# Attention: the value products of a unit in two halves, and the steps behind them one slot later

## The chip, the cores and the metric

The kernel runs on one core of a Trainium2 chip. The metric is the device time of one execution in microseconds; the kernel before was run three times.

## The reference

The input is `x` of 8 x 512 x 256 and a context of the same shape. Four blocks follow each other, each added to `x`: an mLSTM mixing block over 4 heads, a GELU network, a cross-attention over 16 heads of 64, and a router with 8 experts. The change lies in the attention:

```python
q = query @ W_Query + B_Query          # 256 -> 1024, 16 heads of 64
k = key @ W_Key + B_Key
v = value @ W_Value + B_Value
scores = jnp.einsum('bqhd,bkhd->bhqk', q, k) / D ** 0.5
probs = jax.nn.softmax(scores, axis=-1)
out = jnp.einsum('bhqk,bkhd->bqhd', probs, v)
return out.reshape(B, Lq, H * D) @ W_Output + B_Output
```

The query is the normalized `x`, key and value are the context.

## The kernel before

`attention` (from line 827) works in 64 units `u`, one for each pair of heads of each of the 8 batches (HP = 8 pairs a batch). A unit has 2 heads x 4 tiles of 128 query rows, so 8 row tiles, and an iteration of the loop over `u` has 8 slots `j`, one for each. There are 65 iterations: each engine's program runs the same double loop, with the later steps of unit u - 1 and the first steps of unit u + 1 beside the slots of unit u. The order of each engine's queue is written out by hand in these loops, and an engine works its queue in order.

What a slot j of iteration u does, by engine:

- **TensorE.** `score(u, j)`: two matmuls of 512 columns (line 958), into one of two PSUM banks. `turn(u, j - 2)`: four transposes (line 969) of the scaled row tile two slots back, into one of two banks; slots 0 and 1 do those of tiles 6 and 7 of unit u - 1. Then, by slot: 0 and 1, `project(u + 1, ...)` of queries and keys (line 937); 2, all of `weigh_values(u - 1)` (line 979); 4, `project_values(u + 1)` (line 946); 5 and 6, a half each of `output(u - 1, ...)` (line 989). `weigh_values` multiplies, for each of 4 key tiles and 2 heads, a 128 x 64 block of values with 512 columns of turned probabilities; the heads go to the two halves of the columns of the array and of one bank (O_BANK). Each f32 matmul is two instructions in the trace.
- **VectorE.** `row_sum(u, j - 1)` (a reciprocal, line 1158), `row_max(u, j)` (line 1153), `keep(u, j - 2)` (line 1165, a copy of the turned tile out of PSUM), and by slot: 1, the second part of the queries (line 1140, two instructions); 2, that of the keys (line 1147); 7, both halves of `add_out(u - 1, ...)` (line 1172), which add the output products to x. Half 1 of the output shares O_BANK with the value products.
- **ScalarE.** The exponential of tile j with its row sum (line 1093); queries in slot 0 and keys in slot 1, out of PSUM; `heads_out` in slot 4, before the exponential (line 1070); `values` in slot 5 (line 1065); and the copies of turned tiles 4 and 5 in slots 6 and 7 (line 1112).
- **GpSimd.** It multiplies each row tile with its reciprocal (line 1128).
- **SyncE.** After each unit's keys it issues four transfers that copy the keys between partitions (line 913).

So a row tile passes this chain: score, row maximum (VectorE), exponential (ScalarE), reciprocal (VectorE), scaling (GpSimd), turn (TensorE).

From the second batch on, four iterations of each eight (u % 8 = 1 to 4, u >= 8) also treat the batch that is done. NORM (1): VectorE takes statistics, one tile in each of slots 2 to 5. APPLY (2): VectorE normalizes, one tile in each of slots 2 to 5. TURN (3): TensorE transposes in slots 3 and 7; ScalarE copies the first part in slot 4 and the second in slot 0 of the next iteration, after the exponential. GATE (4): TensorE multiplies with the gate weights in slots 3 and 7, and `project` of the keys in slot 1 waits for the second of those copies (semaphore `xT`), as it writes the same bank. The last batch is treated after the loop.

The waits of TensorE's steps, as far as they matter: `turn(u, j)` waits for the scaled tile (`pn`) and for a free bank; `score(u, j)` for exponential j - 2; `weigh_values(u - 1)` for all turned tiles of its unit and for the last addition that read O_BANK (`x`).

Of the kernel before, what the change touches and what calls it, by code (L numbers as in the profile page):

```python
# [24 lines left out]
TPB = S // P  # L25
# [338 lines left out]
def wait_count(eng, sem, value):  # L364

    if value > 0:
        eng.wait_ge(sem, value)
# [459 lines left out]
def attention(nc, c, x_all, xnT_all, ctxT_all, first, Wq, Wk, Wv, Wo, gate_w, lg, rows, rows_in, out, landed):  # L827

    U = HP * B
    NBL = 2 * TPB  # L830
    with ExitStack() as ctx:
# [8 lines left out]
        V = sb("V", [P, 2, TPB, P], F32)  # L840
# [24 lines left out]
        def there(u):  # L865
            return 0 <= u < U
# [15 lines left out]
        def wait_turned_copies(eng, u, n):  # L882

            wait_count(eng, s["pt_v"], u * BY_DVE[NBL] + BY_DVE[n])
            wait_count(eng, s["pt_a"], u * BY_ACT[NBL] + BY_ACT[n])

        with nc.Block() as block:
# [32 lines left out]
            def _(pe):  # L920
# [49 lines left out]
                                           c["ident"][:, :])  # L970
                    ins.then_inc(s["t_ps"], 1)

                def weigh_values(u):
                    wait_turned_copies(pe, u, NBL)
                    pe.wait_ge(s["V"], u + 1)
                    wait_count(pe, s["x"], 2 * u)
                    for t in range(TPB):
                        for h in range(2):
                            ins = pe.matmul(ps[AD * h:AD * h + AD, O_BANK, :], V[:, u % 2, t, AD * h:AD * h + AD],  # L979
                                            PT[:, u % 2, h, t, :], start=t == 0, stop=t == TPB - 1)  # L980
                    ins.then_inc(s["pv"], 1)

                def output(u, half):
                    if half == 0:
# [32 lines left out]
                for u in range(U + 1):  # L1017
                    for j in range(NBL):
                        if there(u):
                            score(u, j)  # L1020
                            if j >= 2:
                                turn(u, j - 2)
                        if j < 2 and there(u - 1):
                            turn(u - 1, NBL - 2 + j)
                        if j < 2 and there(u + 1):
                            project(u + 1, j)
                        if j == 2 and there(u - 1):
                            weigh_values(u - 1)
                        if j == 4 and there(u + 1):
                            project_values(u + 1)  # L1030
                        if j in (5, 6) and there(u - 1):
                            output(u - 1, j - 5)
                        if j in (3, 7) and there(u):
                            if j == 3 and there(u + 1) and u % HP in (TURN, GATE):
                                pe.wait_ge(s["kl"], u + 2)
                            if routed(u, TURN) is not None:
                                turn_rows(routed(u, TURN), j // 4)
                            if routed(u, GATE) is not None:
                                if routed(u, GATE) == 0 and j == 3:
                                    pe.wait_ge(s["gT"], 16 * DC)  # L1040
                                map_gates(routed(u, GATE), j // 4)
# [6 lines left out]
            def _(act):  # L1048
# [36 lines left out]
                values(0)  # L1085
                for u in range(U + 1):
                    for j in range(NBL):
                        if j == 4 and there(u - 1):
                            heads_out(u - 1)
                        if there(u):  # L1090
                            act.wait_ge(s["nmax"], NBL * u + j + 1)
                            wait_count(act, s["t_ps"], NBL * u + j - 3)
                            act.activation(Pr[:, j % 4, :], ps[:, S_BANK + j % 2, :], ACT.Exp,  # L1093
                                           bias=nmax[:, j % 4:j % 4 + 1], accum_out=rsum[:, j % 4:j % 4 + 1]
                                           ).then_inc(s["exp"], 1)
                        if j == 4 and routed(u, TURN) is not None:
                            keep_rows(routed(u, TURN), 0)
                        if j == 0 and routed(u, TURN + 1) is not None:
                            keep_rows(routed(u, TURN + 1), 1)
                        if j == 0 and routed(u, GATE + 1) is not None:  # L1100
                            keep_logits(routed(u, GATE + 1))
                        if there(u + 1):
                            if j == 0:
                                queries(u + 1)
                            if j == 1:
                                keys(u + 1)
                            if j == 5:
                                values(u + 1)
                        if there(u) and j - 2 in ON_ACT:
                            act.wait_ge(s["t_ps"], NBL * u + j - 1)  # L1110
                            q = P * ((j - 2) % TPB)
                            act.copy(PT[:, u % 2, (j - 2) // TPB, :, q:q + P],
                                     ps[:, T_BANK + j % 2, :].rearrange("p (t q) -> p t q", t=TPB)
                                     ).then_inc(s["pt_a"], 1)
# [20 lines left out]
            def _(dve):  # L1135
# [72 lines left out]
                for u in range(U + 1):  # L1208
                    for j in range(NBL):
                        if there(u):  # L1210
                            if j >= 1:
                                row_sum(u, j - 1)
                            row_max(u, j)
                            if j >= 2:
                                keep(u, j - 2)
                        if j < 2 and there(u - 1):
                            keep(u - 1, NBL - 2 + j)
                        if there(u + 1):
                            if j == 1:
                                queries(u + 1)  # L1220
                            if j == 2:
                                keys(u + 1)
                        if 2 <= j < 2 + TPB and routed(u, NORM) is not None:
                            take_stats(routed(u, NORM), j - 2)
                        if j == 2 + TPB and routed(u, NORM) is not None:
                            finish_stats(routed(u, NORM))
                        if 2 <= j < 2 + TPB and routed(u, APPLY) is not None:
                            apply(routed(u, APPLY), j - 2)
                        if j == 7:
                            if there(u):  # L1230
                                row_sum(u, j)
                            if there(u - 1):
                                if u > 1:
                                    dve.wait_ge(s["x"], 2 * (u - 1))
                                add_out(u - 1, 0)
                                add_out(u - 1, 1)
                for t in range(TPB):
                    take_stats(LAST, t)
                finish_stats(LAST)
# [500 lines left out]
```

## Time and profile before

| | us |
|---|---|
| runs | 1843.49, 1844.89, 1848.96 |
| median | 1844.89 |
| span of the profiled execution | 1843.2 |
| TensorE busy | 1663.1 (90%) |
| VectorE busy | 1209.8 (66%) |
| ScalarE busy | 843.8 (46%) |
| GpSimd busy | 608.1 (33%) |

The page gives only the span of the profiled execution, from first to last instruction; its own time was not taken apart from it. The attention stage takes from about 437 to 1655 us. In rows of a timeline stand the start, the time covered, the engine, the line and operation, the tiles, and how many instructions the row merges; in brackets is the engine's idle time before the first and what ended it. PE is the matmuls and PEld the weight loads of TensorE, DVE is VectorE, ACT ScalarE, POOL GpSimd. An instruction can start while the one before it on its engine ends, so the distance between starts is what an instruction costs its engine.

### The profile page before, as it was taken

The page shows a single profiled execution, that of the slowest core. Times are in us where ns is not written, and L with a number is a line of the kernel's source. Part 1 is how long each engine was busy: PE and PEld are TensorE (multiplying, and loading weights), DVE is VectorE, ACT ScalarE, POOL GpSimd, SP SyncE. Part 2 cuts the span into 40 slices and gives each one's busy share as a digit, 9 for nine tenths or more (in the row PEclk, how much of TensorE's full clock was granted, in tenths as well). Part 3 has the DMA queues.
Part 4 walks back from the last instruction along what each step waited for, and adds up shares of the span by engine and source line. Part 5 has one row for each costly group of instructions (what it writes and reads, how often), then busy time and mean ns, then how long its engine had stood idle before and what let it go on. Part 6 is the DMA issues. An engine that isn't in the chain of part 4 may idle for free. (4 is left out here: it accounts for less than half of the span.)

```text
span 1843.2 us, 25796 instructions
## 1 busy us (share of the span) xinstructions
PE 1663.1 (90%) x8789; PEld 1128.1 (61%) x8789; DVE 1209.8 (66%) x2689; ACT 843.8 (46%) x1870; POOL 608.1 (33%) x730
## 2 busy tenths in 40 slices
PE   6569999996999999999999999999999999973584
PEld 4447777754666666666666666666666766642352
DVE  6445656532777777776776776776777677757761
ACT  3324343431555555555555555555555555531110
POOL 2143445430333323332332332333232323220375
PEclk9669999997999999999999999999999999985697
DMA  8100000003323232323232322222223223213254
GB/s 254 27 23 12 12 12 1 1 0 106 69 47 69 47 92 46 69 69 69 47 92 47 67 72 61 54 65 74 56 60 79 59 53 86 46 45 99 44 85 58
DMA packets 68961, 109.46 MB, mean 59 GB/s; under 512 B 18400, under 2 KB 50400, under 8 KB 68832
## 3 DMA queue, kind: packets, MB, share of 16 engines
q1 hardware_dynamic: 62688, 99.29, 22.1%
q0 software_dynamic: 6144, 8.52, 3.0%
q8 instruction: 72, 1.18, 0.3%
q14 instruction: 57, 0.47, 0.1%
HBM read 27.84 MB, written 12.85 MB: 22 GB/s over the span
## 5 line engine op out<-in xcount | busy, mean ns | idle before, releaser
L1128 POOL TENSOR_SCALAR at_Pr<-at_Pr,at_rinv 128x512 f32<-128x512 f32 x512 | 355.8, 695 | 841.2 <-DVE at_rinv L1158 841.2
L1093 ACT ACTIVATE at_Pr<-at_ps,at_nmax 128x512 f32<-128x512 f32 x512 | 352.2, 688 | 535.2 <-DVE at_nmax L1153 533.6
L1153 DVE TENSOR_REDUCE at_nmax<-at_ps 128x1 f32<-128x512 f32 x512 | 351.2, 686 | 154.0 <-PE at_ps L958 142.5
L958 PE MATMUL at_ps<-at_k,at_q 128*128 128x512 f32 x1024 | 420.7, 492 | 10.8 <-DMA at_k<-at_k_own 9.1
L969 PE MATMUL at_ps<-k_ident,at_Pr 128*128 128x128 f32 x2048 | 309.8, 274 | 4.5 <-POOL at_Pr L1128 4.5
L969 PEld LDWEIGHTS at_ps<-k_ident,at_Pr 128*128 128x128 f32 x2048 | 250.5, 140 | 90.2 <-POOL at_Pr L1128 27.7
L1165 DVE COPY at_PT<-at_ps 128x512 f32<-128x512 f32 x384 | 261.4, 681 | 0.0
L958 PEld LDWEIGHTS at_ps<-at_k,at_q 128*128 128x128 f32 x1024 | 174.6, 191 | 130.7 <-issue 121.2
L979 PE MATMUL at_ps<-at_PT,at_V 128*64 128x512 f32 x1024 | 235.4, 602 | 0.9 <-DVE at_PT L1165 0.9
L1158 DVE RECIPROCAL at_rinv<-at_rsum 128x1 f32<-128x1 f32 x512 | 83.3, 163 | 161.1 <-ACT at_Pr L1093 159.1
L979 PEld LDWEIGHTS at_ps<-at_PT,at_V 128*64 128x64 f32 x1024 | 68.1, 137 | 122.5 <-issue 121.4
L989 PE MATMUL at_ps<-at_wo,at_oT 128*128 128x256 f32 x512 | 131.6, 380 | 0.8 <-ACT at_oT L1070 0.8
L459 PE MATMUL mm_ps<-mx_w,mm_hT 128*128 128x256 f32 x512 | 119.6, 382 | 0.0
L449 PE MATMUL mm_ps<-m_xnT,mx_w 128*128 128x512 f32 x256 | 112.6, 598 | 1.3 <-ACT m_xnT L598 1.3
L937 PE MATMUL at_ps<-m_ctxT,at_w_rest 128*128 128x512 f32 x224 | 105.9, 595 | 4.0 <-ACT m_xnT L1075 4.0
L946 PE MATMUL at_ps<-at_w_rest,m_ctxT 128*128 128x128 f32 x896 | 109.2, 275 | 0.0
L937 PE MATMUL at_ps<-m_xnT,at_w_rest 128*128 128x512 f32 x224 | 107.1, 601 | 0.0
L946 PEld LDWEIGHTS at_ps<-at_w_rest,m_ctxT 128*128 128x128 f32 x896 | 104.5, 192 | 0.0
L459 PEld LDWEIGHTS mm_ps<-mx_w,mm_hT 128*128 128x128 f32 x512 | 94.3, 190 | 16.1 <-issue 3.8
L1140 DVE SCALAR_TENSOR_TENSOR at_q<-at_ps,m_b_all,at_q 64x512 fp32r<-64x512 f32 x128 | 96.0, 750 | 11.0 <-ACT at_q L1053 8.2
L1093 ACT ACTIVATION_READ_ACCUMULATOR at_Pr<-at_ps,at_nmax 128x1 f32 x512 | 98.5, 192 | 0.0
L989 PEld LDWEIGHTS at_ps<-at_wo,at_oT 128*128 128x128 f32 x512 | 87.4, 190 | 8.3 <-ACT at_oT L1070 1.7
(236 smaller groups left out, 1996.5 us busy)
## 6 DMA issues: line engine op xcount, KB each, us to landing
at_k<-at_k_own SPq DMA_DIRECT2D x256, 256.0 KB, 4.3
k_x<-in_x SPq DMA_DIRECT2D x8, 512.0 KB, 8.5
mg_ctx<-in_ctx SPq DMA_DIRECT2D x8, 512.0 KB, 8.7
mx_ctxn<-in_ctx SPq DMA_DIRECT2D x8, 512.0 KB, 3.8
rows<-m_ctxT SPq DMA_DIRECT2D x16, 256.0 KB, 2.6
out<-k_x SPq DMA_DIRECT2D x8, 512.0 KB, 3.5
r_w<-in_L_ffn_w SPq DMA_DIRECT2D x16, 256.0 KB, 5.5
mx_w<-in_L_ffn_w SPq DMA_DIRECT2D x2, 1024.0 KB, 10.0
```

The source lines that it names most:

```text
L449: ins = pe.matmul(ps[:, H_BANK + f % 4, :], w1_s[:, k, P * f:P * f + P], xnT_all[:, k, b * S:b * S + S], start=k == 0, stop=k == DC - 1)
L459: ins = pe.matmul(ps[:, Y_BANK + t // 2, D * (t % 2):D * (t % 2) + D], hT[:, f, P * t:P * t + P], w2_s[:, f, :], start=f == 0, stop=f == F ...
L937: ins = pe.matmul(ps[:, A_BANK + k, :], weights(k, d, hp), src[:, d, b * S:b * S + S], start=d == 0, stop=d == DC - 1)
L946: ins = pe.matmul(ps[:, A_BANK, P * t:P * t + P], ctxT_all[:, d, b * S + P * t:b * S + P * t + P], weights(2, d, hp), start=d == 0, stop=d ...
L958: ins = pe.matmul(ps[:, S_BANK + j % 2, :], q2[:, u % 2, h, q:q + P], k2[:, u % 2, h, part, :], start=part == 0, stop=part == 1)
L969: ins = pe.transpose(ps[:, T_BANK + j % 2, P * t:P * t + P], Pr[:, j % 4, P * t:P * t + P], c["ident"][:, :])
L979: ins = pe.matmul(ps[AD * h:AD * h + AD, O_BANK, :], V[:, u % 2, t, AD * h:AD * h + AD], PT[:, u % 2, h, t, :], start=t == 0, stop=t == TP ...
L989: ins = pe.matmul(ps[:, Y_BANK - half, D * (t % 2):D * (t % 2) + D], oT[:, P * t:P * t + P], wo_s[:, u % HP, :], start=True, stop=True)
L1093: act.activation(Pr[:, j % 4, :], ps[:, S_BANK + j % 2, :], ACT.Exp, bias=nmax[:, j % 4:j % 4 + 1], accum_out=rsum[:, j % 4:j % 4 + 1]).th ...
L1128: pool.tensor_scalar(Pr[:, n % 4, :], Pr[:, n % 4, :], rinv[:, n % 4:n % 4 + 1], 1.0, ALU.mult, ALU.mult).then_inc(s["pn"], 1)
L1153: dve.tensor_reduce(nmax[:, j % 4:j % 4 + 1], ps[:, S_BANK + j % 2, :], AX.X, ALU.max, negate=True).then_inc(s["nmax"], 1)
L1165: dve.tensor_copy(PT[:, u % 2, j // TPB, :, q:q + P], ps[:, T_BANK + j % 2, :].rearrange("p (t q) -> p t q", t=TPB)).then_inc(s["pt_v"], 1)
```

## The change

The value products of unit u - 1 are made in two halves: key tiles 0 and 1 in slot 2, tiles 2 and 3 in slot 4. (The short name counts slots from 1.) The value projection goes from slot 4 to slot 5, the halves of the output products from slots 5 and 6 to 6 and 7. ScalarE's `heads_out` goes to slot 5 and `values` to slot 6. VectorE's second addition to x goes from the end of slot 7 to slot 0 of the next iteration, behind the row maximum and the copy of a turned tile there.

```diff
--- before.py
+++ after.py
@@ -970,15 +970,17 @@
                                            c["ident"][:, :])
                     ins.then_inc(s["t_ps"], 1)
 
-                def weigh_values(u):
-                    wait_turned_copies(pe, u, NBL)
-                    pe.wait_ge(s["V"], u + 1)
-                    wait_count(pe, s["x"], 2 * u)
-                    for t in range(TPB):
+                def weigh_values(u, half):
+                    if half == 0:
+                        wait_turned_copies(pe, u, NBL)
+                        pe.wait_ge(s["V"], u + 1)
+                        wait_count(pe, s["x"], 2 * u)
+                    for t in (2 * half, 2 * half + 1):
                         for h in range(2):
                             ins = pe.matmul(ps[AD * h:AD * h + AD, O_BANK, :], V[:, u % 2, t, AD * h:AD * h + AD],
                                             PT[:, u % 2, h, t, :], start=t == 0, stop=t == TPB - 1)
-                    ins.then_inc(s["pv"], 1)
+                    if half:
+                        ins.then_inc(s["pv"], 1)
 
                 def output(u, half):
                     if half == 0:
@@ -1024,12 +1026,12 @@
                             turn(u - 1, NBL - 2 + j)
                         if j < 2 and there(u + 1):
                             project(u + 1, j)
-                        if j == 2 and there(u - 1):
-                            weigh_values(u - 1)
-                        if j == 4 and there(u + 1):
+                        if j in (2, 4) and there(u - 1):
+                            weigh_values(u - 1, j // 4)
+                        if j == 5 and there(u + 1):
                             project_values(u + 1)
-                        if j in (5, 6) and there(u - 1):
-                            output(u - 1, j - 5)
+                        if j in (6, 7) and there(u - 1):
+                            output(u - 1, j - 6)
                         if j in (3, 7) and there(u):
                             if j == 3 and there(u + 1) and u % HP in (TURN, GATE):
                                 pe.wait_ge(s["kl"], u + 2)
@@ -1085,7 +1087,7 @@
                 values(0)
                 for u in range(U + 1):
                     for j in range(NBL):
-                        if j == 4 and there(u - 1):
+                        if j == 5 and there(u - 1):
                             heads_out(u - 1)
                         if there(u):
                             act.wait_ge(s["nmax"], NBL * u + j + 1)
@@ -1104,7 +1106,7 @@
                                 queries(u + 1)
                             if j == 1:
                                 keys(u + 1)
-                            if j == 5:
+                            if j == 6:
                                 values(u + 1)
                         if there(u) and j - 2 in ON_ACT:
                             act.wait_ge(s["t_ps"], NBL * u + j - 1)
@@ -1233,7 +1235,11 @@
                                 if u > 1:
                                     dve.wait_ge(s["x"], 2 * (u - 1))
                                 add_out(u - 1, 0)
-                                add_out(u - 1, 1)
+                        if j == 0 and there(u - 2):
+                            wait_count(dve, s["x"], 2 * (u - 2))
+                            add_out(u - 2, 1)
+                dve.wait_ge(s["x"], 2 * (U - 1))
+                add_out(U - 1, 1)
                 for t in range(TPB):
                     take_stats(LAST, t)
                 finish_stats(LAST)
```

## Rows read from the trace of the kernel before

**Rows 1.** The page: span, and the granted clock in 40 slices.

```profile
span 1843.2 us, 25796 instructions
...
PEclk9669999997999999999999999999999999985697
```

**Rows 2.** Waits, 457 to 1650 us: total us, times, longest.

```profile
PEld at_ps L969 <- POOL at_Pr L1128: 27.7, 57, 1.2
...
PE at_ps L937 <- ACT m_xnT L1075: 4.0, 7, 0.6
```

**Rows 3.** Timeline of the weight loads, iteration 37: start, us, engine, line [idle before].

```profile
1142.22 0.59 PEld L969 LDWEIGHTS at_ps<-k_ident,at_Pr 128*128 128x128 f32 x4
...
1144.84 0.59 PEld L969 LDWEIGHTS at_ps<-k_ident,at_Pr 128*128 128x128 f32 x4
1145.60 0.20 PEld L979 LDWEIGHTS at_ps<-at_PT,at_V 128*64 128x64 f32 x4 [0.17 <-issue]
...
1148.22 0.14 PEld L979 LDWEIGHTS at_ps<-at_PT,at_V 128*64 128x64 f32 x2 [0.28 <-issue]
1149.18 0.30 PEld L958 LDWEIGHTS at_ps<-at_k,at_q 128*128 128x128 f32 x2 [0.81 <-issue]
1149.52 0.59 PEld L969 LDWEIGHTS at_ps<-k_ident,at_Pr 128*128 128x128 f32 x4
...
1150.42 0.59 PEld L969 LDWEIGHTS at_ps<-k_ident,at_Pr 128*128 128x128 f32 x4
...
1156.66 0.59 PEld L969 LDWEIGHTS at_ps<-k_ident,at_Pr 128*128 128x128 f32 x4
...
1157.93 0.42 PEld L969 LDWEIGHTS at_ps<-k_ident,at_Pr 128*128 128x128 f32 x4 [0.41 <-POOL at_Pr L1128]
...
1160.38 0.59 PEld L969 LDWEIGHTS at_ps<-k_ident,at_Pr 128*128 128x128 f32 x4
```

**Rows 4.** Timeline of VectorE, iterations 37 and 38.

```profile
1156.85 0.16 DVE L1158 RECIPROCAL at_rinv<-at_rsum 128x1 f32<-128x1 f32 x1 [0.84 <-ACT at_Pr L1093]
1157.09 0.69 DVE L1153 TENSOR_REDUCE at_nmax<-at_ps 128x1 f32<-128x512 f32 x1
1158.63 0.16 DVE L1158 RECIPROCAL at_rinv<-at_rsum 128x1 f32<-128x1 f32 x1 [0.84 <-ACT at_Pr L1093]
1158.71 1.29 DVE L1172 TENSOR_TENSOR k_x<-at_ps,k_x 128x512 f32<-128x512 f32 x2
1159.91 0.68 DVE L1153 TENSOR_REDUCE at_nmax<-at_ps 128x1 f32<-128x512 f32 x1
...
1161.52 0.67 DVE L1153 TENSOR_REDUCE at_nmax<-at_ps 128x1 f32<-128x512 f32 x1
...
1166.43 0.15 DVE L1158 RECIPROCAL at_rinv<-at_rsum 128x1 f32<-128x1 f32 x1
```

**Rows 5.** Timeline of ScalarE, iteration 37, slots 5 to 7.

```profile
1154.95 0.58 ACT L1065 COPY at_V<-at_ps 128x512 f32<-128x512 f32 x1
...
1157.82 0.69 ACT L1093 ACTIVATE at_Pr<-at_ps,at_nmax 128x512 f32<-128x512 f32 x1 [0.52 <-DVE at_nmax L1153]
```

**Rows 6.** Timeline of GpSimd, iteration 37, slot 6.

```profile
1157.18 0.69 POOL L1128 TENSOR_SCALAR at_Pr<-at_Pr,at_rinv 128x512 f32<-128x512 f32 x1 [1.07 <-DVE at_rinv L1158]
```

**Rows 7.** Timeline of the weight loads, iteration 36 (GATE), slots 1 and 2.

```profile
1121.66 0.59 PEld L969 LDWEIGHTS at_ps<-k_ident,at_Pr 128*128 128x128 f32 x4
...
1125.10 0.14 PEld L969 LDWEIGHTS at_ps<-k_ident,at_Pr 128*128 128x128 f32 x1
```

**Rows 8.** Timeline of VectorE, iteration 33 (NORM), slot 2.

```profile
1072.54 0.42 DVE L1177 BATCH_NORM_STATS2 at_stats<-k_x 128x6 f32<-128x256 f32 x1
1072.87 0.15 DVE L1158 RECIPROCAL at_rinv<-at_rsum 128x1 f32<-128x1 f32 x1
```

**Rows 9.** Timeline of VectorE, iteration 63, row maxima 3 and 7.

```profile
1631.07 0.69 DVE L1153 TENSOR_REDUCE at_nmax<-at_ps 128x1 f32<-128x512 f32 x1 [2.66 <-PE at_ps L958]
...
1637.48 0.68 DVE L1153 TENSOR_REDUCE at_nmax<-at_ps 128x1 f32<-128x512 f32 x1
```

## The prediction

> **What bounds the kernel now.** The page comes first: a span of 1843.2 us and a TensorE clock that is full through the attention stage [rows 1]. Then the list of waits over that stage: TensorE waits for another engine in two places that recur, the transposes of line 969 for GpSimd's scaled rows (57 times) and the projection of line 937 for ScalarE (7 times) [rows 2]. Then the weight loads of one iteration in order of time [rows 3]. A load starts as the matmul before it starts, so they are TensorE's clockwork. I call M(j) the start of the first load of the transposes in slot j (slots count from 0, as j does); it is also the start of the second score matmul. M(1) of iteration 37 is 1142.22, M(1) of iteration 38 is 1160.38: a unit takes 18.16 us. TensorE's queue is in order and nearly full, so I first ask what its own work comes to, and where it stands still.
>
> - Slot 3, score and turn alone: 1150.42 - 1149.52 = 0.90. Slot 1, with a projection: 1144.84 - 1142.22 = 2.62, so a projection is 1.72.
> - Slot 2, with the value products: M(3) - M(2) = 4.68, of which 3.78 beyond score and turn. Its eight pairs of loads are 0.14 busy + 0.28 idle apart, near 0.43 a pair, 3.42 together. So 0.36 is neither score, turn nor product. It lies at the two ends of the block: its first load waits 0.17, and the first score load after it comes 0.96 after the last pair's load, 0.81 idle, where 0.43 would do [rows 3].
> - Slots 7 and 0: M(7) = 1156.66, so M(0) is 1157.56; from M(7) to M(1) pass 3.72 where 0.90 + 2.62 = 3.52 is work. The missing 0.20 is the wait for GpSimd: the load of 1157.93 comes 0.37 after M(0) [rows 3]. A load late by 0.37 costs 0.20, so 0.17 of lateness is free.
> - In the iteration that transposes and gates a finished batch, M(2) - M(1) is 3.44 instead of 2.62 [rows 7]: the projection waits 0.82 for ScalarE's copy of a transposed row block.
>
> The row chain of the other engines decides when a scaled row is there. From slot 7 [rows 3 to 6]: M to row maximum 0.43 (1157.09), to exponential 0.73 (1157.82), to reciprocal 0.81 (1158.63), to GpSimd 0.33 (1156.85 to 1157.18), to the load 0.75 (1157.93). Together 3.05.
>
> **The change, part by part.**
>
> 1. **The block of value products becomes two.** The products are the same, 16 loads and matmuls. The second half stands in slot 4, with slot 3's score and turn between. What a block costs beyond its pairs is paid twice: +0.36 in each of iterations 1 to 62 (iteration 64 has no scores, so its halves touch; iteration 63 is in part 5): 62 x 0.36 = **+22.1**. Nothing hides it, since TensorE sets the pace. Bounds: 0 (if the 0.36 came from something that the first block alone meets) and 0.36. I take 0.36, as it stands at the two edges and a half block has both.
>
> The rows show a load that starts only when the matmuls of the other tile width are over. The Trainium skill, TensorEngine Tiling (Array Packing), section Key Properties, says that changing the tiling mode drains TensorE; by that rule this change adds two drains per unit. The page has no price for one; by the rule the trace agrees, and with the rows' 0.36 the sum is unchanged.
>
> 2. **Output products move from slots 5, 6 to 6, 7; the value projection from 4 to 5.** No instruction is added. M(0) now follows M(7) by 0.90 + 0.87 (an output half is 0.85 to 0.88 by the same sort of difference) instead of 0.90. Row 6 is scaled at M(6) + 3.05, M(0) is at M(6) + 3.54: the wait for GpSimd goes. It exists in iterations 2 to 63 except 14, those that follow TensorE's batch work in slot 7, which hides it (the 57 of the list [rows 2] hold those of iterations 0, 1, 63 and 64 too): 48 x 0.20 = **-9.6**. Bounds: 0 to -9.6.
>
> 3. **The second addition of the output moves behind row maximum 0 of the next unit.** Two additions take 1158.71 to 1159.91, 0.60 each [rows 4]. ScalarE now copies the values (0.58 [rows 5]) between exponentials 6 and 7, ahead of a PSUM copy of the same size: 0.68 + 0.60 + 0.60 = 1.88 against a slot of 1.77, so exponential 7 is 0.11 late. Row maximum 0 then starts at M(7) + 0.43 + 0.73 + 0.11 + 0.81 + 0.08 + 0.60 = M(7) + 2.76 = M(0) + 0.99; now it is at 1159.91, M(0) + 2.35. It and what hangs on it come 1.36 earlier, more than the 0.82 of the ScalarE wait: 7 x 0.82 = **-5.7**. Bounds: 0 to -5.7.
>
> 4. **What is late next.** Slots 2 to 4 were 4.68 + 0.90 + more; now the turn of slot 4 stands at M(1) + 2.62 + 2.07 + 0.90 + 0.90 = M(1) + 6.49, with 2.07 for half a block and its ends. Before, it had 1.71 more. It needs row 2: VectorE goes from row maximum 1 (1161.52) to reciprocal 2 (1166.43) without a pause, 4.91, through the queries' and the keys' second halves. In the new order, row maximum 1 is ready at M(1) + 0.43 and VectorE free for it at M(0) + 0.99 + 0.61 + 0.62 + 0.60 + 0.19 = M(0) + 3.01, that is M(1) + 0.39. So the load can start at M(1) + 0.43 + 4.91 + 0.33 + 0.75 = M(1) + 6.42: 0.07 in hand, 0.24 with the free lateness. No wait in plain units. In the two iterations per batch in which VectorE also takes statistics or normalizes, such a step before reciprocal 2 adds 0.33 (1072.54 to 1072.87 [rows 8]): 0.26 late by the load, about 0.10 in cost, 14 x 0.10 = **+1.4**. Bounds: 0 and 14 x 0.33 = 4.6. Value products, scores and output products wait for things that are there over 1 us earlier; the keys' DMAs, issued by SyncE after the keys' second half, have half a unit as before. No queue but TensorE's, ScalarE's and VectorE's is passed.
>
> 5. **The last unit.** With nothing to project, iteration 63 goes at the row chain's pace: from one row maximum to the next 0.73 + 0.81 + 0.08 = 1.62. Its whole block holds row maximum 3 back to 1631.07 [rows 9]. By halves it comes at 1629.35; slot 4 then takes 0.90 + 2.97, row maximum 5 is at 1633.22, maxima 6 and 7 follow at about 1.60 to 1636.42, against 1637.48 [rows 9]: **-1.1**. Bounds: 0 to -1.9. Iteration 0 has no products; its moved projection fits under the same chain: 0.
>
> **Sum:** 22.1 - 9.6 - 5.7 + 1.4 - 1.1 = +7.1, minus about 0.4 because the block's ends read as 0.356: **+6.7**. Against the profiled span that gives 1843.2 + 6.7 = 1849.9. The median of the runs, 1844.89, lies 1.7 above the span; I keep that: **1851.6 us**, 0.36% slower. A difference of 0.3%, 5.5 us, is about what a measurement of this kernel can tell from none.
>
> **Rivals.**
>
> - **Faster: the block's ends are not paid twice.** If the 0.36 were a wait that the first half meets and the second doesn't, the first term goes: 1851.6 - 22.1 = 1829.5. For it: the wait is put down to "issue", not to a cause. Against: the same idle time stands before and after the block in every unit, also in iteration 63, where the data is long there. Chance 0.08.
> - **One end only is paid again** (about half of 0.36): 1840.6, within 0.3%. No row speaks for it; it is the case in between. Chance 0.06.
> - **Slower by more: the row chain becomes the bound in slot 4.** Place: the turn of row 2. It decides from a slip of 0.28 on VectorE ahead of row maximum 1 (0.04 there, 0.24 behind). If ScalarE's moved copy held exponential 7 back by its whole 0.58, not 0.11, the slip is 0.47 and the load 0.20 too late in 35 plain units, and 0.43 more in the 14 with a VectorE step; the 14 with TensorE batch work in slot 3 have room. 7.0 + 6.0 = +13: 1864.6. For it: 0.24 is thin, and six VectorE steps stand in the sum. Against: each is from a row and VectorE's pace varies by hundredths. Chance 0.16.
> - **The waits stay in part**: terms 2 and 3 half delivered, +7.6, 1859. Chance 0.06.
>
> **How the numbers follow.** The forecast has 0.64. Its own range, 1848 to 1856, takes the bounds of parts 4 and 5, half of part 3, and the 1 or 2 us by which medians of three differ; as its centre is only 1.2 above the line of 0.3%, about a third of it falls within. Slower: 0.64 x 0.64 + 0.16 + 0.06 = 0.63. Same: 0.23 + 0.06 = 0.29. Faster: 0.08. The range leaves out the faster case, the one-end case and a part of the late chain: 1845 to 1862.
>
> **What the profile would show.** Right: two groups of value products a unit, in slots 2 and 4, each with an idle load at its start (0.17) and before the score behind it (0.81); period 18.32 in plain units; no wait of line 969 for GpSimd at M(0); no wait of line 937 for ScalarE; row maximum 0 about 1.0 after M(0). Wrong: a load of line 969 in slot 4 released by GpSimd in most units (late chain), or a period under 18.16, with the block's ends below 0.36.

## The result and the profile after

| | before | after |
|---|---|---|
| median, us | 1845.01 (6 runs, 1843.49 to 1848.96) | 1850.48 (6 runs, 1847.88 to 1853.23) |
| span of the profiled execution | 1843.2 | 1849.0 |

The ratio is 1.003, with an interval of 1.0018 to 1.0041: slower, by 3.3 to 7.6 us. The middle, 5.5 us, lies on the 0.3% that the prediction took for about the least difference that can be told from none. The forecast was 1851.6. The profiled execution took 1850.7, also 1.7 more than its span.

The page of the kernel after, for [rows 1]. TensorE's clock is full through the attention stage. The row before has an 8 in one slice near the end of that stage where this one has a 9; the section on the hardware comes back to it:

```profile
span 1849.0 us, 25859 instructions
...
PEclk9659999997999999999999999999999999995697
```

The weight loads of iteration 37 and the start of 38, in order of time, as in [rows 3]:

```profile
1148.23 0.59 PEld L969 LDWEIGHTS at_ps<-k_ident,at_Pr 128*128 128x128 f32 x4
...
1150.85 0.59 PEld L969 LDWEIGHTS at_ps<-k_ident,at_Pr 128*128 128x128 f32 x4
1151.61 0.20 PEld L980 LDWEIGHTS at_ps<-at_PT,at_V 128*64 128x64 f32 x4 [0.17 <-issue]
...
1153.47 0.30 PEld L958 LDWEIGHTS at_ps<-at_k,at_q 128*128 128x128 f32 x2 [0.81 <-ACT at_Pr L1095]
1153.82 0.59 PEld L969 LDWEIGHTS at_ps<-k_ident,at_Pr 128*128 128x128 f32 x4
...
1154.73 0.59 PEld L969 LDWEIGHTS at_ps<-k_ident,at_Pr 128*128 128x128 f32 x4
1155.48 0.20 PEld L980 LDWEIGHTS at_ps<-at_PT,at_V 128*64 128x64 f32 x4 [0.17 <-issue]
...
1157.35 0.30 PEld L958 LDWEIGHTS at_ps<-at_k,at_q 128*128 128x128 f32 x2 [0.81 <-ACT at_Pr L1095]
1157.69 0.59 PEld L969 LDWEIGHTS at_ps<-k_ident,at_Pr 128*128 128x128 f32 x4
...
1162.15 0.60 PEld L969 LDWEIGHTS at_ps<-k_ident,at_Pr 128*128 128x128 f32 x4
...
1163.92 0.59 PEld L969 LDWEIGHTS at_ps<-k_ident,at_Pr 128*128 128x128 f32 x4
...
1166.55 0.59 PEld L969 LDWEIGHTS at_ps<-k_ident,at_Pr 128*128 128x128 f32 x4
```

M(1) to M(1) is 1166.55 - 1148.23 = 18.32. Two blocks of value products stand in the unit, and each has 0.17 idle at its entry and 0.81 before the score load behind it, the same figures as the one block of [rows 3]. The 0.81 is now put down to ScalarE's exponential, where it was put down to "issue"; the idle time is the same to the hundredth and the exponential that the score waits for was over more than 1 us before, so the name is the tool's choice and the gap is the block's exit. M(7) to M(0) is 1163.92 - 1162.15 = 1.77, and the load at M(0) has no idle time before it: the wait for GpSimd is gone.

The waits of the attention stage, for [rows 2]: total us, times, longest.

```profile
PEld at_ps L958 <- ACT at_Pr L1095: 107.1, 143, 0.8
...
PEld at_ps L969 <- POOL at_Pr L1130: 11.1, 23, 1.2
```

The second row was 27.7 us in 57 waits. The row of the projection waiting for ScalarE's `m_xnT` (4.0 us, 7 times) is no longer there. In iteration 36 (GATE) the loads that were 3.44 apart [rows 7] are now 2.62 apart, which is the dense figure:

```profile
1128.15 0.59 PEld L969 LDWEIGHTS at_ps<-k_ident,at_Pr 128*128 128x128 f32 x4
...
1130.77 0.59 PEld L969 LDWEIGHTS at_ps<-k_ident,at_Pr 128*128 128x128 f32 x4
```

VectorE at the turn from iteration 37 to 38, for [rows 4]:

```profile
1164.13 0.16 DVE L1160 RECIPROCAL at_rinv<-at_rsum 128x1 f32<-128x1 f32 x1 [0.84 <-ACT at_Pr L1095]
1164.21 0.69 DVE L1174 TENSOR_TENSOR k_x<-at_ps,k_x 128x512 f32<-128x512 f32 x1
1164.82 0.68 DVE L1155 TENSOR_REDUCE at_nmax<-at_ps 128x1 f32<-128x512 f32 x1
...
1166.01 0.68 DVE L1174 TENSOR_TENSOR k_x<-at_ps,k_x 128x512 f32<-128x512 f32 x1
1166.61 0.16 DVE L1160 RECIPROCAL at_rinv<-at_rsum 128x1 f32<-128x1 f32 x1
1166.99 0.69 DVE L1155 TENSOR_REDUCE at_nmax<-at_ps 128x1 f32<-128x512 f32 x1 [0.23 <-PE at_ps L958]
```

Row maximum 0 is at M(0) + 0.90 (forecast 0.99), and VectorE even stands still for 0.23 ahead of row maximum 1. The order could start that row maximum at 1166.69, if reciprocal 0 is followed as closely as in the first two of these rows (0.08), and it starts at 1166.99: 0.30 in hand there, where the forecast had 0.04.

ScalarE in slot 7 of iteration 37, for [rows 5]:

```profile
1163.32 0.69 ACT L1095 ACTIVATE at_Pr<-at_ps,at_nmax 128x512 f32<-128x512 f32 x1
```

Exponential 7 starts 0.73 after row maximum 7 (1162.59), as before. The two copies ahead of it fit into the slot.

**Where the time went**, by marks that both traces have (row maximum 0 of iteration 0; M(2) of iteration 1; M(0) of iteration 63; the last `heads_out`). The places of M(0) of iteration 63 are worked out from dense slots where a wait stands in front.

| stretch | before | after | difference |
|---|---|---|---|
| start to row maximum 0 of iteration 0 | 456.89 | 458.43 | +1.5 |
| to M(0) of iteration 63, by way of M(2) of iteration 1 | to 1621.16 | to 1630.35 | +7.7 |
| to the last `heads_out` | 25.76 | 21.90 | -3.9 |
| to the end | 196.3 | 196.8 | +0.5 |

So the attention itself gave +3.8, and the two stretches that the change doesn't touch +2.0. The middle stretch is what parts 1 to 4 were about (22.1 - 9.6 - 5.7 + 1.4 = 8.2, against 7.7).

### The profile page after: what moved, and what is told of

It is laid out like the page before. It is cut to its first block and busy times, and to the rows that moved or that the text cites. A ratio compares the mean times of both kernels' runs of the same rounds, so it can differ in the third digit from the quotient of the medians.

```text
span 1849.0 us, 25859 instructions
## 1 busy us (share of the span) xinstructions
PE 1675.8 (91%) x8789; PEld 1129.0 (61%) x8789; DVE 1211.1 (65%) x2689; ACT 863.8 (47%) x1870; POOL 608.3 (33%) x730
## 5 line engine op out<-in xcount | busy, mean ns | idle before, releaser
L958 PEld LDWEIGHTS at_ps<-at_k,at_q 128*128 128x128 f32 x1024 | 173.1, 190 | 179.6 <-ACT at_Pr L1095 107.1
L980 PE MATMUL at_ps<-at_PT,at_V 128*64 128x512 f32 x1024 | 247.7, 605 | 0.9 <-DVE at_PT L1167 0.9
L980 PEld LDWEIGHTS at_ps<-at_PT,at_V 128*64 128x64 f32 x1024 | 62.2, 136 | 95.8 <-issue 94.7
L937 PE MATMUL at_ps<-m_xnT,at_w_rest 128*128 128x512 f32 x224 | 107.1, 601 | 0.0
L1055 ACT ACTIVATE at_q<-at_ps,m_b_all 64x512 fp32r<-64x512 f32 x128 | 87.6, 685 | 22.5 <-PE at_ps L937 21.7
```

Of the source, the lines that this page charges most:

```text
L937: ins = pe.matmul(ps[:, A_BANK + k, :], weights(k, d, hp), src[:, d, b * S:b * S + S], start=d == 0, stop=d == DC - 1)
L958: ins = pe.matmul(ps[:, S_BANK + j % 2, :], q2[:, u % 2, h, q:q + P], k2[:, u % 2, h, part, :], start=part == 0, stop=part == 1)
```

## Experiments

The names M(j), unit and block are those of the prediction. "Plain" is a unit in which no finished batch is treated. All ratios are against the kernel before, run beside the kernel in question.

**e1, the block whole again, the rest of the change kept.**

```diff
-                        if j in (2, 4) and there(u - 1):
-                            weigh_values(u - 1, j // 4)
+                        if j == 2 and there(u - 1):
+                            weigh_values(u - 1, 0)
+                            weigh_values(u - 1, 1)
```

> Theory A (TensorE sets the pace and every block of value products costs 0.36 us at its ends): the kernel after, with both halves side by side in slot 2 again. A plain unit takes 18.32 - 0.36 = 17.96 us, 0.20 less than before, because the wait for GpSimd at the end of the unit stays away; the median comes to about 1828 us, 0.9% faster than before. Theory B (the loss comes from the other moves: the value projection, the copies on ScalarE, the addition on VectorE): it stays at 1848 us or more, with plain units near 18.3 us.

Measured: 1882.85, ratio 1.0207 (1.0193 to 1.0221), plain unit 19.03. Neither theory had this. The weight loads of iteration 38:

```profile
1173.50 0.59 PEld L969 LDWEIGHTS at_ps<-k_ident,at_Pr 128*128 128x128 f32 x4
...
1176.54 0.42 PEld L969 LDWEIGHTS at_ps<-k_ident,at_Pr 128*128 128x128 f32 x4 [0.76 <-POOL at_Pr L1131]
```

These are M(3) and the first load of the transposes in slot 5, which turn row 3. It comes 3.04 after M(3), which is the row chain of 3.05 that the prediction worked out. With the block whole in slot 2 and the value projection in slot 5, slots 3 and 4 hold nothing but score and turn, so a dense M(5) would be M(3) + 1.80 = 1175.30. The load is 1.24 late, 0.17 of it free: 1.07 per unit, and 17.96 + 1.07 = 19.03. What follows: the second half in slot 4 is not only a cost. It is the work that lets the value projection stand in slot 5. From here on I had a third theory, C: *TensorE's work in two neighbouring slots j and j + 1, beyond score and turn, must be at least 3.05 - 0.17 - 1.80 = 1.08, or the turn of row j waits for the rest.*

**e2, the halves alone**, in slots 2 and 3 of the kernel before; nothing else is moved.

```diff
-                        if j == 2 and there(u - 1):
-                            weigh_values(u - 1)
+                        if j in (2, 3) and there(u - 1):
+                            weigh_values(u - 1, j - 2)
```

> The kernel before with nothing but the value products cut in two, in slots 2 and 3. Theory A: plain units 18.16 + 0.36 = 18.52 us, the wait of line 969 for GpSimd unchanged, about 1866 us. Theory B: cutting costs nothing, and as the other engines are fed sooner the time is 1845 us or less.

Measured: 1867.32, ratio 1.0122 (1.0107 to 1.0138). The plain unit is 18.50 to 18.51, so +0.345 against the kernel before. The weight loads of one iteration:

```profile
1158.80 0.59 PEld L969 LDWEIGHTS at_ps<-k_ident,at_Pr 128*128 128x128 f32 x4
...
1161.77 0.59 PEld L969 LDWEIGHTS at_ps<-k_ident,at_Pr 128*128 128x128 f32 x4
...
1164.74 0.59 PEld L969 LDWEIGHTS at_ps<-k_ident,at_Pr 128*128 128x128 f32 x4
...
1172.24 0.42 PEld L969 LDWEIGHTS at_ps<-k_ident,at_Pr 128*128 128x128 f32 x4 [0.41 <-POOL at_Pr L1130]
```

M(2) to M(3) and M(3) to M(4) are 2.97 each, 0.90 and 2.07. The second block costs as much at its ends as the first, and the wait at M(0), which this kernel has no reason to lose, is there. Both rivals in which the ends are not paid twice fall.

**e3, three pieces** instead of two: key tile 0, key tile 1, tiles 2 and 3, in slots 2, 3 and 4 of the kernel after.

```diff
-                    for t in (2 * half, 2 * half + 1):
+                    for t in ((0,), (1,), (2, 3))[piece]:
...
-                        if j in (2, 4) and there(u - 1):
-                            weigh_values(u - 1, j // 4)
+                        if j in (2, 3, 4) and there(u - 1):
+                            weigh_values(u - 1, j - 2)
```

> The kernel after with the value products in three pieces, in slots 2, 3 and 4. Theory A: one more pair of ends per unit, plain units 18.32 + 0.36 = 18.68 us, about 1871 us. Theory B: no change against the kernel after, 1850 us.

Measured: 1870.68, ratio 1.0139 (1.0124 to 1.0155). The plain unit is 1180.81 - 1162.15 = 18.66, +0.34 on the kernel after:

```profile
1162.15 0.59 PEld L969 LDWEIGHTS at_ps<-k_ident,at_Pr 128*128 128x128 f32 x4
...
1163.92 0.30 PEld L958 LDWEIGHTS at_ps<-at_k,at_q 128*128 128x128 f32 x2 [0.81 <-issue]
...
1166.02 0.30 PEld L958 LDWEIGHTS at_ps<-at_k,at_q 128*128 128x128 f32 x2 [0.81 <-issue]
...
1168.99 0.30 PEld L958 LDWEIGHTS at_ps<-at_k,at_q 128*128 128x128 f32 x2 [0.81 <-ACT at_Pr L1095]
...
1180.81 0.59 PEld L969 LDWEIGHTS at_ps<-k_ident,at_Pr 128*128 128x128 f32 x4
```

Three blocks, three exits of 0.81, and the third price equals the second. The NORM and APPLY units are 18.66 too: with slot 4 later by 0.34 their turn has nothing to wait for, so the term of part 4 is gone here.

**e4, the moved addition alone**, in the kernel before.

```diff
                                 add_out(u - 1, 0)
-                                add_out(u - 1, 1)
+                        if j == 0 and there(u - 2):
+                            wait_count(dve, s["x"], 2 * (u - 2))
+                            add_out(u - 2, 1)
+                dve.wait_ge(s["x"], 2 * (U - 1))
+                add_out(U - 1, 1)
```

> The kernel before with nothing but the second addition moved behind row maximum 0. Theory A: plain units stay at 18.16 us, since TensorE's wait for GpSimd lies ahead of it; the projection's wait for ScalarE goes from 0.82 to about 0.23 us, 7 times, and the last unit starts 0.6 us earlier: 4 to 5 us less, about 1840.5 us. Theory B (the addition is what VectorE pays for): 1850 us or more.

Measured: 1840.67, ratio 0.9978 (0.9969 to 0.9987), plain unit 18.16. In iteration 36 the two loads of [rows 7] are 2.83 apart, so 0.21 of the 0.82 is left:

```profile
1122.14 0.59 PEld L969 LDWEIGHTS at_ps<-k_ident,at_Pr 128*128 128x128 f32 x4
...
1124.97 0.59 PEld L969 LDWEIGHTS at_ps<-k_ident,at_Pr 128*128 128x128 f32 x4
```

By itself this part of the change is a gain.

**e5, both additions together in slot 7**, the rest of the change kept.

```diff
                                 add_out(u - 1, 0)
-                        if j == 0 and there(u - 2):
-                            wait_count(dve, s["x"], 2 * (u - 2))
-                            add_out(u - 2, 1)
-                dve.wait_ge(s["x"], 2 * (U - 1))
-                add_out(U - 1, 1)
+                                add_out(u - 1, 1)
```

> The kernel after with both additions in slot 7 again, ahead of row maximum 0. Theory A (TensorE's queue bounds, and VectorE ahead of reciprocal 2 has 0.24 us in hand): VectorE comes 0.16 us later to row maximum 1; plain units stay at 18.32 us, the two units per batch with a VectorE step of their own go from 18.42 and 18.39 to about 18.55, and the last unit starts 0.6 us later: 2 to 3 us more than the kernel after, about 1853 us. Theory B (the moved addition carries the kernel after): over 1858 us, with plain units above 18.4 us.

Measured: 1852.18, ratio 1.0037 (1.0023 to 1.005). The plain unit is 18.32 as expected. The NORM and APPLY units are 18.41 each (18.41 and 18.39 in the kernel after), and not 18.55: the slack of 0.30 ahead of row maximum 1, which the trace of the kernel after already showed, takes up the later row maximum 0. This run's attention stage is 2.3 longer than that of the kernel after (1655.77 - 459.69 against 1652.25 - 458.43), of which 1.7 is the last block of value products at half clock, treated below. The rest, about 0.6, is all that the moved addition gives in the kernel after.

That is little against the gain in e4, and the GATE iteration says why. In iteration 36 the loads of [rows 7] are 2.62 apart here too:

```profile
1129.58 0.59 PEld L969 LDWEIGHTS at_ps<-k_ident,at_Pr 128*128 128x128 f32 x4
...
1132.20 0.59 PEld L969 LDWEIGHTS at_ps<-k_ident,at_Pr 128*128 128x128 f32 x4
```

ScalarE's wait is gone without the moved addition. Half of the output products now stands in slot 7, between M(7) and M(0), so M(0) comes 0.87 later against the chain that leads to row maximum 0. In iteration 36 row maximum 0 is at M(0) + 1.91 in the kernel before, + 1.04 in e5, + 1.31 in e4 and + 0.44 in the kernel after. The wait was 0.82: the 0.87 of e5 removes all of it, the 0.60 of e4 leaves 0.21.

**e6, VectorE held up in slot 0.** The kernel after with one more reduction of 512 columns in slot 0, behind the copy of the turned tile.

```diff
+        extra = sb("extra", [P, 1], F32)
...
+                        if j == 0 and there(u - 1):
+                            dve.tensor_reduce(extra[:, :], c["ones_row"][:, :], AX.X, ALU.max)
```

> The kernel after with one more reduction of 128x512 on VectorE (about 0.60 us) in slot 0, ahead of reciprocal 0; its result is not used. Theory A with the slack that the prediction gives (0.28 us): plain units 18.32 + 0.32 = 18.64 us, waiting in slot 4 for GpSimd, the NORM and APPLY units about 18.97; TURN and GATE units unchanged; about 1869 us. Theory B (VectorE is off the path altogether): no change, 1850 us.

Measured: 1856.8, ratio 1.0065 (1.0049 to 1.008). That is 6.3 over the kernel after, where 18.5 was expected. The plain unit is 18.33 to 18.34, only 0.01 to 0.02 over; NORM and APPLY are 18.67, 0.26 to 0.28 over. VectorE, iterations 37 and 38:

```profile
1168.16 0.68 DVE L1240 TENSOR_REDUCE at_extra<-k_ones_row 128x1 f32<-128x512 f32 x1
...
1169.42 0.67 DVE L1156 TENSOR_REDUCE at_nmax<-at_ps 128x1 f32<-128x512 f32 x1
```

and the weight loads there (M(1), and the load of slot 4 that turns row 2):

```profile
1168.70 0.59 PEld L970 LDWEIGHTS at_ps<-k_ident,at_Pr 128*128 128x128 f32 x4
...
1175.39 0.42 PEld L970 LDWEIGHTS at_ps<-k_ident,at_Pr 128*128 128x128 f32 x4 [0.24 <-POOL at_Pr L1131]
```

The reduction takes 0.59 of VectorE (the addition behind it starts at 1168.75), but row maximum 1 slips only from M(1) + 0.44 to M(1) + 0.72, by about 0.3. The load is then 0.19 later than dense (1174.30 + 0.90 = 1175.20). So the late-chain rival had its place and its releaser right, and its threshold wrong: 0.30 ahead of row maximum 1 plus 0.24 behind it, 0.54 in all. The units give 35 x 0.01 + 14 x 0.27 = 4.1 of the 6.3. The last unit gives 2.2: from M(0) of iteration 63 to row maximum 7 pass 16.26, against 14.06 in the kernel after. Of these 2.2, VectorE's chain gives 0.6 (row maximum 2 at M(0) + 4.93, against 4.35). The other 1.6 is not the reduction: the half block in slot 2 of iteration 63 took 3.22 instead of 1.94, at a granted clock of 0.50 (1640 to 1642), treated below.

**e8, the output products alone**, in slots 6 and 7 of the kernel before; block whole, value projection in slot 4, both additions in slot 7.

```diff
-                        if j in (5, 6) and there(u - 1):
-                            output(u - 1, j - 5)
+                        if j in (6, 7) and there(u - 1):
+                            output(u - 1, j - 6)
```

> The kernel before with nothing but the output halves moved to slots 6 and 7 (the block whole in slot 2, the value projection in slot 4). What the first run of the whole block showed gives the rule to test: turn j needs 3.05 - 0.17 = 2.88 us from M(j) to M(j+2), so the work of two neighbouring slots beyond score and turn must be 1.08 us or more. Theory C (this rule): slots 7 and 0 now keep it, slots 5 and 6 (0.87) fall short by 0.21 instead: plain units stay at 18.17 us, with TensorE's wait for GpSimd now in slot 7; the projection's wait for ScalarE goes (7 times 0.82): about 1840 us. Theory A as the prediction had it (the moved output products take away 0.20 per unit): plain units 17.96 us, about 1829 us.

Measured: 1843.55, ratio 0.9989 (0.9979 to 1.0). The plain unit is 18.15, as theory C had it:

```profile
1150.94 0.59 PEld L969 LDWEIGHTS at_ps<-k_ident,at_Pr 128*128 128x128 f32 x4
...
1153.98 0.42 PEld L969 LDWEIGHTS at_ps<-k_ident,at_Pr 128*128 128x128 f32 x4 [0.41 <-POOL at_Pr L1131]
...
1155.58 0.59 PEld L969 LDWEIGHTS at_ps<-k_ident,at_Pr 128*128 128x128 f32 x4
```

The load at M(0) (1155.58) is free, and the same wait of 0.41 now stands in slot 7, 3.04 after M(5): slot 5 is empty and slot 6 has 0.87. Moving the output products by themselves moves the wait by one row and doesn't end it.

The time was expected at about 1840 and came out 3.5 higher, and the rows say why. The wait in slot 7 now stands in the TURN and GATE units too, where TensorE's batch work used to hide it: a TURN unit takes 19.03, against 18.84 in the kernel before. And ScalarE's wait is only shortened: in iteration 36 M(1) to M(2) is 2.89, so 0.27 of the 0.82 is left. Row maximum 0 is at M(0) + 1.37 there, 0.54 earlier than before and not 0.87, as the wait now stands in slot 7, ahead of M(0). Together 14 x 0.20 + 7 x 0.27 = 4.7.

**e9, a version from the rule.** The kernel before with both halves of the output products in slot 6, and the moved addition of e4.

```diff
-                        if j in (5, 6) and there(u - 1):
-                            output(u - 1, j - 5)
+                        if j == 6 and there(u - 1):
+                            output(u - 1, 0)
+                            output(u - 1, 1)
```

> The kernel before with both output halves in slot 6 and the second addition behind row maximum 0; value products whole in slot 2, value projection in slot 4. Theory C: every pair of neighbouring slots has 1.08 us or more, no wait for GpSimd is left, plain units take 17.96 us; with 4 us from the addition the time is about 1830.5 us, faster than both kernels. If instead 18.16 us is a bound of another engine, it stays at 1840.7 us as with the addition alone.

Measured: 1831.61 (1830.22 to 1834.79), ratio 0.9933 (0.9919 to 0.9946). It beats both kernels. The weight loads of one iteration, slots 6 to 0:

```profile
1146.97 0.46 PEld L969 LDWEIGHTS at_ps<-k_ident,at_Pr 128*128 128x128 f32 x4 [0.19 <-POOL at_Pr L1129]
...
1149.47 0.59 PEld L969 LDWEIGHTS at_ps<-k_ident,at_Pr 128*128 128x128 f32 x4
...
1150.56 0.42 PEld L969 LDWEIGHTS at_ps<-k_ident,at_Pr 128*128 128x128 f32 x4 [0.24 <-POOL at_Pr L1129]
```

The plain unit is 17.99 to 18.00, 0.16 under the kernel before. Two loads still wait for GpSimd, but they are late by no more than 0.19 against dense slots (1146.97 against 1145.92 + 0.90, and 1150.56 against 1149.47 + 0.90), and both together leave 0.03 to 0.04 over the 17.96 of work.

That no wait would be left was wrong, and theory C as it stands can't say why: every pair of slots has at least 1.7. The reason is in VectorE's rows of iteration 37, slot 4:

```profile
1144.29 0.16 DVE L1159 RECIPROCAL at_rinv<-at_rsum 128x1 f32<-128x1 f32 x1 [0.25 <-ACT at_Pr L1094]
1144.38 0.67 DVE L1154 TENSOR_REDUCE at_nmax<-at_ps 128x1 f32<-128x512 f32 x1
```

M(4) is 1143.24. Row maximum 4 starts 1.14 after it, not 0.43, because reciprocal 3 stands ahead of it in VectorE's queue and waits for exponential 3. Slot 3 holds only score and turn, so row 4 follows row 3 by 0.91, less than the 1.62 that the row chain needs from one row maximum to the next. The chain of row 4 is thus 3.73 instead of 3.05, and slots 4 and 5 give 3.58: 0.15 late. Slots 6 and 7, behind the bare slot 5, do the same to row 6. Behind a slot with nothing but score and turn, the next pair needs about 1.76 and not 1.08.

## Why the prediction came out right, and which steps failed

The table puts theory C against every kernel: TensorE's work by slot beyond score and turn, the pair of neighbouring slots with the least, what it is short of 1.08, and the blocks. Period is 17.96 for one block without a wait, plus 0.36 for each further block, plus the shortfall. It speaks of plain units only. The kernel before, the kernel after and e1 gave theory C its figures, e2 and e3 test the price of a block, and e8 and e9 were forecast from it before they ran.

| kernel | least pair | short | blocks | period so | measured |
|---|---|---|---|---|---|
| before, e4 | 6 and 7: 0.87 | 0.21 | 1 | 18.17 | 18.16 |
| after, e5, e6 | 6 and 7: 1.74 | none | 2 | 18.32 | 18.32, 18.32, 18.33 to 18.34 |
| e1 | 3 and 4: 0 | 1.08 | 1 | 19.04 | 19.03 |
| e2 | 6 and 7: 0.87 | 0.21 | 2 | 18.53 | 18.50 to 18.51 |
| e3 | 6 and 7: 1.74 | none | 3 | 18.68 | 18.66 |
| e8 | 5 and 6: 0.87 | 0.21 | 1 | 18.17 | 18.15 |
| e9 | 5 and 6: about 1.7 | none | 1 | 17.96 | 17.99 to 18.00 |

- **Part 1 (+22.1)** held: in the kernel after the two blocks take 2.97 + 2.96 - 1.80 = 4.13 beyond score and turn, where the one block took 3.78, so 0.35; 0.345 in e2, 0.34 for the third block in e3. The rule on the tiling mode that the prediction weighed (the Trainium skill, TensorEngine Tiling (Array Packing), section Key Properties) goes the same way, and these runs give it a price here. They don't show that the drain is its whole cause: no run had a block of the other tile width without the gap.
- **Part 2 (-9.6)** held as a sum, but its reason was too small. It said that the wait goes because the output products move. e8 shows that by this alone the same wait turns up one row earlier, in slot 7. In the change the value projection goes to slot 5 as well, and e1 shows that this in turn needs work in slot 4. The three moves are one step, and the working didn't see that: it asked what M(0) needs, and not what every pair of slots needs.
- **Part 3 (-5.7)** held in size, and its sum of 1.36 was near: the GATE iteration has the dense 2.62, and row maximum 0 is at M(0) + 0.90. But the term stands under the moved addition, and e5 has the full gain without it. The 0.87 that the output half puts between M(7) and M(0) is enough by itself; the addition's 0.60 is not (e4). The 0.11 by which exponential 7 was to be late did not come: it starts 0.73 after its row maximum, as before.
- **Part 4 (+1.4)** held in size and failed in its slack. In a NORM iteration of the kernel after the load of slot 4 is 0.27 late against 1077.76 + 0.90, as forecast (0.26), and the next M is 0.10 later than dense:

```profile
1077.76 0.59 PEld L969 LDWEIGHTS at_ps<-k_ident,at_Pr 128*128 128x128 f32 x4
1078.93 0.42 PEld L969 LDWEIGHTS at_ps<-k_ident,at_Pr 128*128 128x128 f32 x4 [0.31 <-POOL at_Pr L1130]
1081.73 0.59 PEld L969 LDWEIGHTS at_ps<-k_ident,at_Pr 128*128 128x128 f32 x4
```

  What failed is "VectorE free at M(1) + 0.39". It is free at about M(1) + 0.14: row maximum 0 comes 0.09 earlier, as exponential 7 is on time, and reciprocal 0 costs the engine 0.08, where I had taken 0.19 from another place of the order; the steps between are shorter by the rest. So 0.04 was 0.30, and the rival that hung on it had too high a chance: it decides from a slip of 0.54, and the whole moved copy of ScalarE, priced at 0.47, would not have reached it. e5 and e6 were both expected too slow for the same reason.
- **Part 5 (-1.1)** failed in size. The last unit goes at the row chain's pace, so what counts there is when its first row maximum starts. From M(0) of iteration 63 to row maximum 7 the kernel before took 1637.48 - 1621.16 = 16.32, the kernel after 1644.41 - 1630.35 = 14.06: -2.3. The term's own steps came true: the block cut in two brings row maximum 3 closer to row maximum 2 by 1.73 (4.35 to 2.62; forecast 1.72), and from there to row maximum 7 it takes 0.68 longer. Missing was that the start of the unit moves too. Row maximum 2 is at M(0) + 5.56 in the kernel before, 5.22 in e4, 4.69 in e5 and 4.35 in the kernel after. So the moved addition gives 0.34 (before to e4, and e5 to after), and the output half in slot 7 gives 0.87, the same 0.87 as in part 3. Part 5 had neither.
- **The sum.** 22.1 - 9.6 - 5.7 + 1.4 - 1.1 is +7.1. The "minus about 0.4 because the ends read as 0.356" was wrong: 62 x 0.356 is already 22.1, so it was taken off twice. The right sum of my own terms was +7.1, or 1852.0.
- **The number.** The medians differ by 5.5 and the forecast said 6.7, which looks better than it is. The profiled attention stage gave +3.8: the steady part +7.7, as forecast within 0.5; the last unit -2.3 for -1.1; and the last block of value products, which no term was about, -1.6. The stretches outside added +2.0, which no step of the change explains. Over the ten kernels, one profile each, row maximum 0 of iteration 0 came between 455.65 (e8) and 460.12 (e4), with the same code ahead of it, and the stretch behind the last `heads_out` took 194.7 to 196.7. Both +1.5 and +0.5 lie within that. So it was luck that the total came within 1.2 of the forecast: in the profiles the attention gave 3.3 less than the +7.1 of the terms, and 2.0 came back by chance. The steps are judged by their periods and not by the total.

## What to carry to other kernels

In an in-order queue that is cut into slots with a result due two slots later, the check is the same for every pair of neighbouring slots: their work must cover the chain of the other engines. That chain is longer behind a bare slot (3.73 against 3.05 in e9) and where another engine has a step of its own (the NORM units of part 4), so take it for each slot from its own rows. A work item moved out of one pair and into another ends one wait and can start a dearer one elsewhere (e1 saves the 0.36 of a block and pays 1.07 in slot 5), so work out all pairs before and after. Two moves that end the same wait don't add up (the moved addition: 3.5 us alone in e4, about 0.6 on top of the other moves), so take the full change back one part at a time as well. Cutting a run of matmuls of another tile width has a price for each block, here 0.34 to 0.36 us; before paying it to fill a slot, look for a step of the usual width that can go there whole, as the output products do in e9.

## What the runs showed of the hardware

- **The blocks of value products at the end run at either clock.** Take the last one. It is the same 16 matmuls, behind the same wait for VectorE. MATMUL rows of the kernel before, and then TensorE's busy time, count and granted clock over its first part (the figure behind the five engines is the clock):

```profile
1641.63 5.24 PE L979 MATMUL at_ps<-at_PT,at_V 128*64 128x512 f32 x16 [0.88 <-DVE at_PT L1165]
```

```profile
1641.60:1645.00 3.40, 3.37 (x10) 1.02 (x12) 0.00 (x0) 0.00 (x0) 0.00 (x0) 0.52 0.02 5
```

  The same two views of the kernel after:

```profile
1648.55 3.65 PE L980 MATMUL at_ps<-at_PT,at_V 128*64 128x512 f32 x16 [0.88 <-DVE at_PT L1167]
```

```profile
1648.50:1652.00 3.50, 3.45 (x16) 1.06 (x16) 0.00 (x0) 0.00 (x0) 0.00 (x0) 1.00 0.00 0
```

  0.52 is about the 1.2 GHz level, 1.00 the 2.4 GHz one. TensorE had been waiting on and off for the row chain in both. Over the ten kernels, with one profile each, the block took 3.65 in after, e1, e3, e6 and e9, and 5.24 to 5.35 in before, e2, e4, e5 and e8; e5 differs from after only in VectorE's order. Whether a given kernel always falls on the same side stays open, since each has one profile. The Trainium skill, TensorE: Matmul & The Clock Gate, section Part 1: The HAM clock gate, says that the point at which the clock changes varies between runs of one kernel; no repeated profile here shows that. The difference is worth 1.6 us, beside the 5.5 between the two medians. The block in slot 2 of iteration 63 does the same: the half block took 1.94 at full clock in the kernel after, and 3.37 in e2 and 3.22 in e6 around a granted clock of 0.50; the whole block took 5.12 in e8. How busy TensorE had been doesn't sort the kernels: in the 4 us before the last block it was busy 1.58 in the kernel before and 2.10 in e5, where the clock fell, and 1.47 in e9, 2.10 in e3 and 2.14 in the kernel after, where it didn't.
- **A load that is late by up to 0.17 to 0.19 costs almost nothing**: 0.01 to 0.02 in e6 for 0.19, 0.03 to 0.04 in e9 for two such loads. Beyond that it costs what is over: 0.10 for 0.27 in the NORM unit, 1.07 for 1.24 in e1.
- **The exit of a block has no fixed name in a list of waits.** The same 0.81 is put down to "issue" in the kernel before and e1, and to ScalarE's exponential in the kernel after, where it makes 107.1 us of "wait" that no faster ScalarE would take away.
